# Order of the weight transfers on the SyncE queue: the up weights of the next step ahead of the down weights of this one

## The reference, cut to what matters

```python
def ffn(x, W1, W2, W3):
    hidden = silu(x @ W1.T) * (x @ W3.T)     # 512 -> 2048 features
    hidden = fwht(hidden)                    # Walsh-Hadamard transform over the 2048
    return hidden @ W2.T                     # 2048 -> 512
x = x + 0.5 * ffn(layernorm(x), W1, W2, W3)
x = x + attention(layernorm(x), wq, wk, wv, wo, inv_freq)
x = x + 0.5 * ffn(layernorm(x), W1, W2, W3)
```

## Time and profile before

| | us |
|---|---|
| median of 3 executions | 2688.82 |
| lowest, highest | 2687.78, 2691.37 |
| the profiled execution | 2686.21 |
| its span, first to last instruction | 2684.4 |
| PE busy, share of the span | 96% |
| DVE busy | 75% |
| ACT busy, POOL busy | 20%, 13% |
| HBM read and written | 402.79 MB, 33.55 MB |
| mean granted TensorE clock, as a share of full speed | 0.985 |

### The profile page before, as it was taken

The page is one execution under the profiler, slowest core; times in us unless marked ns, Lnnn a source line. Parts: engine busy times, 40 slices in busy tenths (PEclk is TensorE's granted clock), DMA queues, the critical chain, the costliest instruction groups (busy, mean ns, idle before and its releaser), DMA issues.

```text
span 2684.4 us, 32324 instructions
## 1 busy us (share of the span) xinstructions
PE 2566.9 (96%) x11328; PEld 2093.5 (78%) x11328; DVE 2012.8 (75%) x2482; ACT 542.2 (20%) x829; POOL 357.0 (13%) x171
## 2 busy tenths in 40 slices
PE   4998989999999999999999999999999999998799
PEld 3777768888888888878888888888788888876687
DVE  8556997777777777877777787777777777779812
ACT  1321221121212212112112221112121121112111
POOL 5033880000000000000000000000000000158400
PEclk7999999999999999999999999999999999999899
DMA  5571441555425553355524555155542555234344
GB/s 189 194 308 56 163 153 52 184 206 184 177 78 188 203 188 141 111 186 204 188 94 161 184 204 187 70 192 199 187 166 99 184 201 190 109 117 157 118 180 164
DMA packets 91642, 437.02 MB, mean 163 GB/s; under 512 B 8896, under 2 KB 15296, under 8 KB 58304
## 3 DMA queue, kind: packets, MB, share of 16 engines
q1 hardware_dynamic: 83616, 420.65, 43.1%
q10 hardware_dynamic: 7968, 15.73, 1.6%
HBM read 402.79 MB, written 33.55 MB: 163 GB/s over the span
## 4 chain that ended last, share of the span: by engine, by line
PE 69%; DMA 13%; DVE 13%; issue 2%; SPq 1%; POOL 1%; ACT 0%; POOLq 0%; ACTq 0%; DVEq 0%
PE gu L316 17%; PE gu L318 16%; PE gu L317 16%; DMA w_up<-up_pairs 12%; PE acc L316 6%; PE acc L318 6%; PE acc L317 6%; DVE mixed L830 2%; DVE prod L231 2%; DVE scores L828 2%; DVE hid L777 1%; PE gu L354 1%; DVE tok L1007 1%; SPq L297 1%; DVE prod L228 1%
## 5 line engine op out<-in xcount | busy, mean ns | idle before, releaser
L316 PE MATMUL gu<-xt,w_up 128*128 128x512 f32 x2048 | 809.5, 395 | 48.8 <-DVE w_up L981 26.5
L317 PE MATMUL gu<-xt,w_up 128*128 128x512 f32 x2048 | 799.8, 391 | 0.0
L318 PE MATMUL gu<-xt,w_up 128*128 128x512 f32 x2048 | 799.0, 390 | 0.0
L316 PEld LDWEIGHTS gu<-xt,w_up 128*128 128x128 f32 x2048 | 385.7, 188 | 161.7 <-DMA w_up<-up_pairs 47.9
L773 DVE TENSOR_TENSOR gated<-gated,gu 128x512 f32<-128x512 f32 x256 | 175.2, 684 | 428.9 <-ACT gated L530 428.9
L318 PEld LDWEIGHTS gu<-xt,w_up 128*128 128x128 f32 x2048 | 385.9, 188 | 81.6
L317 PEld LDWEIGHTS gu<-xt,w_up 128*128 128x128 f32 x2048 | 386.1, 189 | 77.6
L316 PE MATMUL acc<-w_down,hid 128*128 128x512 f32 x960 | 382.5, 398 | 33.3 <-DVE hid L777 33.3
L530 ACT ACTIVATE gated<-gu 128x512 f32<-128x512 f32 x256 | 153.1, 598 | 1243.1 <-PE gu L318 1243.1
L318 PE MATMUL acc<-w_down,hid 128*128 128x512 f32 x960 | 379.0, 395 | 0.0
L317 PE MATMUL acc<-w_down,hid 128*128 128x512 f32 x960 | 378.8, 395 | 0.0
(11 more groups left out here) (103 smaller groups left out, 2200.4 us busy)
## 6 DMA issues: line engine op xcount, KB each, us to landing
w_up<-up_pairs SPq DMA_DIRECT2D x240, 1024.0 KB, 5.9
w_down<-down_pairs SPq DMA_DIRECT2D x240, 512.0 KB, 3.3
up_pairs<-w_up SPq DMA_DIRECT2D x16, 1024.0 KB, 4.9
prod<-up_raw SPq DMA_DIRECT2D x16, 512.0 KB, 6.0
down_pairs<-w_attn SPq DMA_DIRECT2D x4, 2048.0 KB, 10.6
x_in<-x ACTq DMA_DIRECT2D x7, 1024.0 KB, 5.4
out<-x_out ACTq DMA_DIRECT2D x7, 1024.0 KB, 5.5
tok<-attn_raw SPq DMA_DIRECT2D x4, 1024.0 KB, 12.4
```

The costliest lines, as they stand in the source:

```text
L316: nc.tensor.matmul(o, w_hi, m_hi, start=first, stop=False)
L317: nc.tensor.matmul(o, w_hi, m_lo, start=False, stop=False)
L318: return nc.tensor.matmul(o, w_lo, m_hi, start=False, stop=last)
```

## The change

SP's program of loads is written in another order. Each load keeps its own wait, its slot, its size and its semaphore. Before, a block's loads were up 0, down 0, up 1, down 1, up 2, down 2, ... Now they are up 0, up 1, down 0, up 2, down 1, ... up 15, down 14, down 15. That is the order of PE's program. The loop has 7 turns of four loads, with one load ahead of it and three behind it. PE, ACT, DVE and POOL have the same programs as before.

```diff
             def weights(b):
 
-                with sp.Fori(0, HT // 2) as jj:
-                    for u in range(2):
-                        sp.wait_ge(s_up_done, HT * b + 2 * jj + u - 1)
-                        load_up(2 * jj + u, u)
-                        sp.wait_ge(s_down_done, HT * b + 2 * jj + u - 1)
-                        load_down(2 * jj + u, u)
+                n0 = HT * b
+
+                def up_weights(j, u):
+                    sp.wait_ge(s_up_done, n0 + j - 1)
+                    load_up(j, u)
+
+                def down_weights(j, u):
+                    sp.wait_ge(s_down_done, n0 + j - 1)
+                    load_down(j, u)
+
+                up_weights(0, 0)
+                with sp.Fori(0, HT // 2 - 1) as jj:
+                    up_weights(2 * jj + 1, 1)
+                    down_weights(2 * jj, 0)
+                    up_weights(2 * jj + 2, 0)
+                    down_weights(2 * jj + 1, 1)
+                up_weights(HT - 1, 1)
+                down_weights(HT - 2, 0)
+                down_weights(HT - 1, 1)
```

## The result

The new kernel takes 2654.0 us (median, 2653.0 to 2655.7), the kernel before 2688.3 us (four executions, 2683.0 to 2691.4). The ratio is 0.9876, interval [0.9861, 0.9891]. The forecast was 2653.8 us. The profiled execution took 2653.04 us with a span of 2651.3, 33.1 us less than the span before.

What follows compares the result with a forecast made beforehand. PE, 96% busy, was taken to stall on late up loads because SP waited for down parts. Removing 34.98 us of stalls, other terms 0, from the 2688.82 us median gave 2653.8 us, range 2647 to 2666.

Steps and rivals of the forecast that it cites:

- (1): Up loads of steps 3 and later, issued ahead of a down load: slack 2.6 to 5.8 us, waits gone, -34.98 us.
- rival C: Weight loads: order isn't the cause, landing stretches with the time given; 2688.8 us, chance 0.06 including the page's rule.
- (2): SP's loop turn: its extra 0.55 us now falls where SP is waiting anyway; cost 0.
- (3): Down loads behind an up load: landed in no more than 12.7 us with 13.28 us available; cost 0.
- (4): Head of a block: down 1 loads right behind up 2, needed 13.6 us later; cost 0, with 5 us to spare.
- (5): Dense blocks 1 and 14: PE waits for DVE, so arriving sooner means waiting longer; gain 0, at most 8 us.
- What is late next: Even blocks with stalls gone: PE's own spacing, 8.16 us a step, becomes the bound; DVE doesn't.
- rival B: The wait partly returns, through DVE's three-unit steps (10 us) or block heads (7 us): 2664 or 2671 us; chance 0.09.
- D: PE without pauses: clock falls from 2.4 to 1.2 GHz; at 100 us of low clock, 2704 us; chance 0.05.

Runs made afterwards that it cites:

- the dose run: Second try: 10j added waits ahead of the up load of step j, against the new load order issued at the old, later moment; 2693.31 us in one execution.
- chip 2: Chip of later runs: the kernel before, unchanged, takes 2670.8 us (median of 9); the new kernel, unchanged, 2653.06 us, ratio 0.9936.
- first session: The runs of the result, no chip on record: new kernel against the kernel before, 2654.0 and 2688.3 us, ratio 0.9876.
- the order alone: Against the new kernel: up load still ahead of the down load, but both wait for down part j-2, inner loop written out; 2652.84 us, ratio 0.9941.

## Why the prediction was right

**The size and the place.** The step that carried it, undisturbed stretches against measured ones, came out to the last digit: 111.52 us each, 34.98 us in all. The span gave 33.1 because of 0.3 us in the dense blocks and their stages and 1.63 us of lower clock at block 15; the prediction didn't have the latter. The median gave 34.3. That the forecast is within 0.2 us of the result is in part luck: its base, 2688.8, was 0.5 us above the 2688.3 of the result, and its difference, 35.0, was 0.7 us too large.

**(1) The landing budget.** Right. It holds to a tenth in the dose run. The landing of a load with nothing ahead of it, taken from one load, was 4.8 us for nearly all. But the text also said why the loads were late, namely that SP was held by a down part, and gave the loop turn only as what makes every second one late. The runs put the weight elsewhere. With only the turn taken out, the old order loses 0.7 us, where the kernel before loses 16.4 (chip 2) or 35.0 (first session). Its loss needs both the distance and the landing that comes with it: 1.08 + 7.0 is over the budget of 7.84 us, while 1.08 + 5.4 or 0.53 + 7.0 would be under it. I had both landings in hand, 5.4 and 7.2 us for equal loads, and passed the 1.8 us over under rival C. The turn's own 0.55 us are the smaller part of it. Nor are there seven such loads a block in the stretches, but six (steps 4 to 14): the load of up 2 leaves 5 us or more behind a down load, and up 2 opens the stretch. Of these 78 loads 65 were late, and one of an odd step.

**(2), (3) and (4).** The turn is hidden, no wait for `w_down` appears, and the heads lose nothing: up 1 to up 2 is 8.16 us in each block. The slack was larger than needed: the order alone, with 2.7 us less, is as fast. One reading in (4) was off and cost nothing: the longest pair isn't 1.08 + 7.2 = 8.3 us but 1.08 + 8.0 = 9.1, by the worst landing in the earlier trace rows.

**(5) The dense blocks.** Stall time in their stretch was 20.8 and 21.1 us and is 20.9 and 21.2. The 3.8 us of idle under `w_up` went over to the wait for DVE, as said: PE's weight loads wait 19.0 us for it in block 1 instead of 15.6.

**What is late next.** PE's own spacing; without any load the time is the same. DVE's three-unit steps never showed: rival B didn't happen. Of rival C the first half is true, for a gain without the new order is possible; its mechanism isn't, for landings shrank. D fell too: the clock in the stretches is 1.00.

**How far it carries.** The 34 us belong to the first session. On chip 2 the same difference would have been 17 us too large, and nothing in the first trace told me that its 7.0 us could be 6.7 elsewhere. I had left a mere 2 us for the spread between runs.

## What to carry to other kernels

Count the loss in stretches of equal work against an undisturbed one, and not from the idle in a list of waits. Where two loads leave together and one is late, compare the landing of equal loads at their different distances before changing the order; the cause may be a few tenths of a microsecond in the issuing queue, which writing out a loop removes. Issue the load that is due first ahead of the other and by itself: that version felt neither the chip or session, nor the distance, nor 2.7 us of delay, while the kernel before, short by 0.4 us at one load and with 1.9 us to spare at the next, felt all of it.

## What the runs showed of the hardware

**The landing of a 1024 KB load behind a 512 KB load depends on the distance.** The medians are 5.4 us up to 0.6 us, 7.3 to 7.5 us at 0.7 to 0.9 us, 5.8 us at 1.4 us, and 4.8 us alone; single loads at 0.67 us take anything from 5.0 to 8.0. In the reverse order, 512 KB behind 1024 KB, no such distance appears between 0.4 and 1.3 us. A pair is thus through 5.8 us after the first issue at a distance of 0.44, and 8.3 us at 0.8. In the late pair looked at, the last 2 us keep only a tenth to three tenths of the DMA engines' time busy. The fit of the Trainium skill ("DMA: Bandwidth & Descriptors", section "Anatomy of one DMA — SWDGE (gpsimd) path", made for GpSimd's transfers) gives 5.6 us as an estimate for the pair: that agrees with the good distance and not with the bad one.

**It differs between sessions.** At 1.08 us the medians are 7.0 and 6.7 us of 84 loads each, and the stretches of the kernel before lose 35.0 and 16.4 us. Whether the chip does that is open.

**A stall of PE is followed by a slow restart.** The next matmul comes after 0.33 us instead of 0.23, and an up part behind a stall takes 0.14 us more (5.58 instead of 5.44 us, the median of 66 in the first trace), at a granted clock of 1.00. That is about 9 of the 35 us lost.
